# Attention on one core: value sums in two PSUM banks by turns, maximum pieces in one, rotation ahead of the pieces, opening queries in four banks

## The reference, cut to what matters

```python
q = (x @ wq).reshape(b, s, H, QH).transpose(0, 2, 1, 3)
q_nope, q_pe = (q[..., :NOPE], q[..., NOPE:])
...
ckv = ckv * jax.lax.rsqrt(jnp.mean(ckv * ckv, axis=-1, keepdims=True) + EPS)
kv = (ckv @ wkv_b).reshape(b, s, H, NOPE + VD).transpose(0, 2, 1, 3)
k_nope, v = (kv[..., :NOPE], kv[..., NOPE:])
...
q_pe = _rope(q_pe, cos, sin)
k_pe = _rope(k_pe[:, None, :, :], cos, sin)
...
scores = jnp.einsum('bhqd,bhkd->bhqk', qs, ks_) * scale
scores = jnp.where(causal, scores, jnp.finfo(scores.dtype).min)
attn = jax.nn.softmax(scores, axis=-1)
out = jnp.einsum('bhqk,bhkd->bhqd', attn, v)
out = out.transpose(0, 2, 1, 3).reshape(b, s, H * VD)
return out @ wo
```

## Time and profile before

| what | value |
|---|---|
| median of 3 runs | 1399.17 us (1397.67 to 1401.56) |
| profiled execution | 1404.18 us |
| its span, first to last instruction | 1402.4 us |
| mean granted PE clock over the span | 0.933 |
| busy share of PE, PEld, DVE, ACT, POOL | 85%, 63%, 56%, 50%, 68% |
| first attention call | about 493 to 865 us of the span |
| second attention call | about 908 to 1282 us of the span |

### The profile page before, as it was taken

One profiled execution on the slowest core, in us unless ns is written; L12 is line 12 of the kernel. 1 busy time (PEld: TensorE's weight loads), 2 busy tenths in 40 slices (PEclk: granted clock), 3 DMA queues, 4 the chain that ended last, 5 costly groups with the idle time before them and its releaser, 6 DMA issues. The chain is left out here.

```text
span 1402.4 us, 18855 instructions
## 1 busy us (share of the span) xinstructions
PE 1188.5 (85%) x5570; PEld 877.9 (63%) x5625; DVE 789.7 (56%) x1712; ACT 697.6 (50%) x1325; POOL 956.0 (68%) x700
## 2 busy tenths in 40 slices
PE   6983688999995469999999997779999999998797
PEld 5873555555553336767767675746667766677686
DVE  4468722222221756666766672847666676663566
ACT  3220123233321227677776785237777777785242
POOL 2024868888884648778887776648777887777454
PEclk9985889999998569999999999969999999999899
DMA  9449235555555300000000000000000000002001
GB/s 325 135 136 240 90 64 79 81 81 82 79 80 92 118 15 4 5 8 9 8 6 3 1 1 13 8 8 8 1 8 8 9 8 1 1 1 66 1 16 46
DMA packets 66512, 68.22 MB, mean 49 GB/s; under 512 B 15072, under 2 KB 59680, under 8 KB 66304
## 3 DMA queue, kind: packets, MB, share of 16 engines
q1 hardware_dynamic: 48336, 43.36, 10.5%
q0 software_dynamic: 15168, 20.72, 9.5%
q10 hardware_dynamic: 2928, 3.15, 0.7%
HBM read 46.10 MB, written 21.10 MB: 48 GB/s over the span
## 5 line engine op out<-in xcount | busy, mean ns | idle before, releaser
L1529 POOL TENSOR_TENSOR att_prob_lo<-att_prob,att_prob_hi 128x1024 fp32r<-128x1024 f32 (+1 forms) x160 | 347.1, 2174 | 85.7 <-ACT att_prob_hi L1457 85.7
L1358 PE MATMUL all_bank<-att_q_hl,sequence_k_hl 128*128 128x512 f32 (+1 forms) x960 | 257.1, 378 | 0.0
L1381 PE MATMUL all_bank<-att_prob_hi,sequence_v_hl 128*128 128x512 f32 (+1 forms) x640 | 190.4, 379 | 16.8 <-ACT late_oT L1469 15.3
L1450 ACT ACTIVATE att_prob<-all_bank 128x1024 f32<-128x1024 f32 (+1 forms) x160 | 150.0, 938 | 86.0 <-PE all_bank L1364 81.8
L1358 PEld LDWEIGHTS all_bank<-att_q_hl,sequence_k_hl 128*128 128x128 f32 x960 | 172.1, 191 | 28.3
L1341 PE MATMUL all_bank<-sequence_k_hl,att_q_hl 128*128 128x512 f32 (+3 forms) x384 | 170.1, 448 | 8.1 <-DVE att_peak L1577 6.0
L1457 ACT CAST att_prob_hi<-att_prob 128x1024 fp32r<-128x1024 f32 (+1 forms) x160 | 154.3, 964 | 5.1
L1328 PE MATMUL all_bank<-sequence_x_hl,sequence_w_hl 128*128 128x512 f32 x384 | 115.1, 438 | 48.1 <-DVE all_xT L1567 40.5
L917 PE MATMUL all_bank<-early_w_gu,moe_xgT 128*128 x316 | 148.8, 554 | 3.6 <-issue 2.5
L882 POOL DMA_INDIRECT sums<-moe_y,early_slot_far x79 | 125.4, 1588 | 36.3 <-issue 17.8
L1381 PEld LDWEIGHTS all_bank<-att_prob_hi,sequence_v_hl 128*128 128x128 f32 x640 | 112.7, 189 | 41.0 <-issue 22.1
(11 more groups left out here) (245 smaller groups left out, 2175.3 us busy)
## 6 DMA issues: line engine op xcount, KB each, us to landing
sequence_w_raw<-wqk_rows SPq DMA_DIRECT2D x16, 256.0 KB, 2.7
early_w_gu<-in_gate SPq DMA_DIRECT2D x16, 224.0 KB, 5.9
early_w_gu<-in_up SPq DMA_DIRECT2D x16, 224.0 KB, 6.0
early_w_down<-in_down SPq DMA_DIRECT2D x1, 3584.0 KB, 21.4
sums<-early_zero SPq DMA_DIRECT2D x18, 128.0 KB, 3.7
all_xT<-in_xT SPq DMA_DIRECT2D x4, 512.0 KB, 7.7
all_x_tok<-in_x SPq DMA_DIRECT2D x1, 2048.0 KB, 16.4
x_rows<-all_x_tok SPq DMA_DIRECT2D x4, 512.0 KB, 3.0
```

The costliest lines, as they stand in the source:

```text
L1358: nc.tensor.matmul(ps, k_hl[:, ks, j * P:(j + 1) * P], q_hl[n % 2][:, qs, :, i * BW + q0:(i + 1) * BW], start=g == 0, stop=False)
L1381: mm = nc.tensor.matmul(out, v_hl[:, vs, j, :], part[:, u % 3, half * WIDE:half * WIDE + 2 * w].rearrange("p (h m) -> p h m", h=2), start= ...
L1450: nc.scalar.activation(prob[:, u % 2, 0:w], s_ps[u % 2][:, 0:w], ACT.Exp, scale=SCALE).then_inc(prob_sb, 1)
L1529: nc.gpsimd.tensor_tensor(prob_lo[:, u % 3, 0:w], prob[:, u % 2, 0:w], prob_hi[:, u % 3, 0:w].bitcast(F32), ALU.subtract).then_inc(lo_sb, 1)
```

## The change

Four edits in `phase_attention`, with no instruction added or taken away:

- the value sums of the blocks e = n * 4 + i go to banks 4 and 6 by turns, and the wait for ACT's copies is for the block two before;
- the pieces use bank 7 alone, and each waits for the peak of the piece right before;
- in the opening the four query chunks of pair 0 go to banks 0 to 3, without waits; the scores, which use these banks, then wait until all four are rotated;
- DVE no longer swaps the first two items: in steps 0 to 3 the rotation stands ahead of all peaks.

```diff
-        pv_ps, q_ps = bank[:, 4, :], bank[:, 5, :]
-        piece_ps = [bank[:, n, :] for n in (6, 7)]
+        pv_banks = [bank[:, n, :] for n in (4, 6)]
+        q_bank = lambda n, k: bank[:, 5, :] if n else bank[:, k, :]
+        piece_ps = bank[:, 7, :]
...
                 def query(item):
-                    if n * QC + k:
+                    if n:
                         pe.wait_ge(sin_sb, n * QC + k)
...
                 def piece(item):
-                    if n * NP + y >= 2:
-                        pe.wait_ge(peak_sb, n * NP + y - 1)
+                    if n * NP + y >= 1:
+                        pe.wait_ge(peak_sb, n * NP + y)
                     pe.wait_ge(q_hi_sb, n * QC + t // 4 * 2 + h + 1)
-                    ps = piece_ps[y % 2]
+                    ps = piece_ps
...
                 def values(u, half):
                     if half == 0:
                         pe.wait_ge(lo_sb, u + 1)
-                        if jj == 0 and e >= 1:
-                            pe.wait_ge(sums_sb, e)
+                        if jj == 0 and e >= 2:
+                            pe.wait_ge(sums_sb, e - 1)
-                    out = pv_ps.rearrange("p (h m) -> p h m", h=2)[:, :, q0:BW]
+                    out = pv_banks[e % 2].rearrange("p (h m) -> p h m", h=2)[:, :, q0:BW]
...
                 for y in range(8):
                     piece(("piece", 0, y))
+                pe.wait_ge(sin_sb, QC)
                 scores(0, 0)
...
                     n, x, _, _ = at(u)
-                    items = aside(n, x)
-                    if items and items[0][0] == "query":
-                        items[0:2] = items[1::-1]
-                    for item in items:
+                    for item in aside(n, x):
                         beside(item)
```

More of the change, by code:

```diff
@@ L1327, in query @@
                         for kc in range(KC):
-                            mm = nc.tensor.matmul(q_ps, w_hl[:, ws, kc, h * P:(h + 1) * P],
+                            mm = nc.tensor.matmul(q_bank(n, k), w_hl[:, ws, kc, h * P:(h + 1) * P],
                                                   x_hl[:, xs, kc, c * WIDE:(c + 1) * WIDE],
@@ L1467, in sums @@
                         own = last_den[half, :] if e == PAIRS * NB - 1 else den[half, e % 2, :]
-                        nc.scalar.copy(own, pv_ps[LORA:P, cols])
-                        done = nc.scalar.copy(oT[half, n, i * BW:(i + 1) * BW], pv_ps[0:LORA, cols])
+                        nc.scalar.copy(own, pv_banks[e % 2][LORA:P, cols])
+                        done = nc.scalar.copy(oT[half, n, i * BW:(i + 1) * BW], pv_banks[e % 2][0:LORA, cols])
                     done.then_inc(sums_sb, 1)
@@ L1563, in rope @@
                     for i, o in ((LORA + 32, LORA), (LORA, LORA + 32)):
-                        nc.vector.tensor_tensor(swapped[o:o + 32, c % 2], q_ps[i:i + 32], sin[i:i + 32, cols], ALU.mult)
+                        nc.vector.tensor_tensor(swapped[o:o + 32, c % 2], q_bank(n, k)[i:i + 32], sin[i:i + 32, cols], ALU.mult)
                     if c >= 2:
                         dve.wait_ge(q_lo_sb, c - 1)
-                    nc.vector.tensor_tensor(raw[:, c % 2], q_ps, cos[:, cols], ALU.mult).then_inc(sin_sb, 1)
+                    nc.vector.tensor_tensor(raw[:, c % 2], q_bank(n, k), cos[:, cols], ALU.mult).then_inc(sin_sb, 1)
                 def peaks(n, y):
@@ L1571, in peaks @@
                     half, whole = (peak[:, n % 2, a, t // 2, h, t % 2:t % 2 + 1] for a in range(2))
-                    ps = piece_ps[y % 2][:, 0:w]
+                    ps = piece_ps[:, 0:w]
                     dve.wait_ge(max_mm, n * NP + y + 1)
```

## The result

The changed kernel takes 1451.53 us (median of 4 runs, 1448.96 to 1452.66) against 1400.37 us of the kernel before beside it (4 runs): a ratio of 1.0365, 95% interval 1.0341 to 1.0389. It is slower, as forecast, by 51 us where 40 were forecast.

The account below looks back on a forecast made before the run. PE was taken to set the pace. Steady pairs plus 22.8, pair 0 plus 13.4, openings plus 7 and last pairs minus 3 gave plus 40 us: 1444 from the profiled 1404.2, a median of 1439, range 1412 to 1458.

Parts of the forecast that it names:

- The single losses: Steady pair: each piece waits for the peak before; 5.7 us lost against 3.8 won, plus 1.9 a pair, 22.8 in all.
- Pair 0: First pair of each call, with more pieces in steps 0 to 2: plus 6.7 us each, plus 13.4 for two.
- The opening: Before pair 0's steps: first peak 4.7 us earlier, then 16 pieces through one bank; plus 3.5 us each, 7 for both.
- The last pair: No queries or next pieces; regains sums' waits but waits for POOL's low parts: minus 1.5 us each, minus 3.
- The two banks for the sums: Values of a steady pair: sums get a block's time to be copied, so waits of 0.45 and 0.78 us go.
- The pieces' waits are covered: Rival: in steps 4 to 9 the 2.7 us of piece waits vanish; 1392 us, chance 0.08.
- The clock falls: Rival: PE's longer stands make one step of each of 14 pairs run at 1.2 GHz; 1490 us, chance 0.06.
- Much faster: Rival: the rotations' waits go and no new one comes; minus 55 us, 1344 us, chance 0.01.
- The weight loads: If PE pulled weight loads ahead for waiting pieces, losses of 0.08 us each would go: 12 us, median 1427.

Follow-up runs that it names:

- the opening kept busy: The changed kernel with added matmuls that nobody reads, filling PE's waits in the opening: 1437.6 us, ratio 1.0256 to the kernel before.
- The fifth run: The kernel before with pieces in one bank and value sums in banks 4 and 6, opening's queries and DVE's order as before: 1474.8 us, ratio 1.0532.
- one piece bank alone: The kernel before with the pieces in bank 7 only, each waiting for the peak before; sums and DVE's order as before: 1481.3 us, ratio 1.0591.
- the first run: The kernel before with one edit, DVE taking the rotation ahead of the pieces' peaks, pieces still in two banks: 1361.4 us, ratio 0.9733.
- the run with both edits: The kernel before with the rotation ahead and the opening's queries in four banks, pieces still in two banks: 1351.7 us, ratio 0.9663.
- the best kernel: The kernel before with rotation ahead and four opening banks: 1351.7 us; with added matmuls that nobody reads in its opening: 1345.7 us, ratio 0.9611.

## Why the prediction was right, and where its sizes were off

**Direction and mechanism** held. PE bounds the attention, the waits for the rotation and for the sums went, and the pieces' waits took their place. I took 1439 us; measured 1451.5, inside 1412 to 1458.

**The single losses** came out as priced. The rule, 0.34 us plus the peak from one piece's place to the next, gave 1.55 for piece 22 and 1.39 for piece 2. In the rows after, piece 22 stands at 633.87 where it could have stood at 632.42 (632.19 plus 0.23), and with 0.09 for its start that is 1.54; piece 2 gives 1.34. The twelve losses of that pair, read the same way, add up to 5.8 us, forecast 5.7. Set matmul by matmul beside the kernel before, they are 6.0, mostly since a start after a wait costs 0.10 to 0.11 rather than 0.09, and 3.9 are won: the pair is longer by 2.1 us instead of 1.9. The start of the rotation 0.04 us after the query's row, for which the prediction names, is not in those rows, where a peak stands between; in the rows after it is 0.04 (631.08 to 631.12). Over 12 pairs: plus 25.7 for a forecast of 22.8.

**Pair 0** was forecast at plus 6.7 and came at 8.8 and 7.5. The term left out the clock. With the opening kept busy pair 0 takes 51.4 us in both calls, plus 7.1; of the 1.6 us between in the first call the query at 0.58 is 1.3.

**The opening** is the term that was mis-sized: plus 3.5 a call in the text, 6.5 and 5.4 measured. The profiles divide the first call's 6.5. The first peak comes 14.1 us after the first query instead of 19.5, minus 5.4, a little better than the forecast's minus 4.7. From there to the scores of step 1 the pieces through one bank and the scores of step 0 take 20.4 us (505.17 to 525.56) instead of 10.5; the text had 19.2 (507.8 to 527). The scores of step 1, to which the text gave nothing, take 4.8 instead of 2.7, plus 2.1, at a clock of 0.53 instead of 1.00. The end of the first peak after, and windows of the scores of step 1, before and after:

```profile
505.17 0.14 DVE L1579 DVE_READ_ACCUMULATOR2_ANT att_peak<- 128x1 f32 x1
...
523.26:525.96 2.70, 2.70 (x14) 1.69 (x14) 0.73 (x4) 1.92 (x5) 1.17 (x1) 1.00 0.00 0
...
525.56:530.36 4.80, 4.80 (x14) 2.85 (x14) 0.55 (x2) 2.35 (x6) 0.00 (x0) 0.53 0.00 0
```

The text gave a range too, plus 1 for the full clock and plus 6 for the low one. At the low clock plus 6.5 and 5.4 were measured, and the opening kept busy (clock 1.00 from 499 us on) is plus 0.5 in the first call and minus 1.7 in the second. The step that failed is the choice between the ends, and the count that stopped where the scores of step 1 begin. The rows showed 0.50 in the opening before, the change makes PE idle more there, and I still took the middle.

**The last pair** was forecast at minus 1.5 and came at minus 1.8 and 1.9. The three waits for the sums are gone, and holding back for POOL was right: the values of step 8 now wait 1.02 us for the low parts, where before those of step 9 waited 0.75.

**The two banks for the sums** were credited with 1.23 us a steady pair, in a sum that was right. The fifth run shows that beside one piece bank and the old order they give nothing there. In the sum this did no harm, since I counted the pieces' losses with the sums' waits already gone. The terms as measured are 25.7, 16.3, 11.9 and minus 3.7, against 22.8, 13.4, 7 and minus 3.

**The rivals.** "The pieces' waits are covered" fell: the steady pair is over 43.8 us, and it is so with one piece bank alone. "The clock falls" is half right. In the steady pairs, with idle times of up to 1.28 us in brackets, the granted clock stays at 1.00, so the mechanism I gave it is not there. But in the opening and in pair 0 it does fall, and it costs 14 us. The rule of the Trainium skill on banks in a cycle ("TensorE: Matmul & The Clock Gate", section "A second HAM failure mode: psum-queue depth-cycling") says that the clock can swing where PE goes through banks with short idle times between groups of matmuls. In the steady pairs, which have them, the trace goes against it. The opening (0.50 and 0.68 between pieces) agrees only in part: PE idles up to 6.2 us at a time there, and the clock is 0.50 in the opening with two banks too. "Much faster" fell. Its number was for the change as a whole; its mechanism, that the queries' waits go and nothing comes, is what the first run does, for 38 us.

**The weight loads**: the rule of the Trainium skill that PE pulls weight loads ahead of matmuls in flight ("TensorE: Matmul & The Clock Gate", section "Step-by-step: what each phase is for") would have made it 12 us less. The rows decide against it here. The weight load of piece 22 stands at 633.87, as its matmul does, though PE had been idle 1.28 us, and the matmul behind it follows 0.11 us later than behind the same piece where no piece waits (the run with both edits):

```profile
633.87 0.19 PEld L1342 LDWEIGHTS all_bank<-sequence_k_hl,att_q_hl 128*128 128x128 f32 x1 [1.72 <-DVE att_peak L1582]
```

## What to carry to other kernels

A bank taken from a buffer that two engines hand to each other is not free because nobody waits there now: price the way from one use to the next (here 0.34 us plus the reader's time) against what stands between them, for every place in the list, and again for every edit that moves the reader. An edit's worth depends on its neighbours: the rotation ahead was worth 38 us with two piece banks and 14 with one, so try the parts alone before the bundle. Where an engine that sets the pace idles in an opening, look at its clock there, and take the price at the clock that the rows show, down to the stretch where they show the full one again.

## What the runs showed of the hardware that I had not expected

Work that nobody reads made a kernel faster. The 73 matmuls of 512 bf16 columns in each opening took the granted clock from 0.50 to 1.00 and the time from 1451.5 to 1437.6 us. In the best kernel 30 of them shortened the openings of the profile by 2.3 and 3.6 us; its total moved by 6 us, which the intervals don't separate.

The low clock reached into a stretch where PE was busy without a break: the query of 3.08 us at 537.42 ran at 0.58, after six microseconds in which PE was busy 4.29 at a clock of 0.99. With the opening kept busy that query took 1.74 us.
